# New orders and slots for the tiles of the first two images in a two-layer attention kernel

## The chip, the cores and the metric

The kernel runs on one core of a Trainium2 chip. Its metric is the device time of one execution in microseconds, the median of several runs. Five engines work from queues of their own, each in its written order: TensorE (PE; PEld are its weight loads), VectorE (DVE), ScalarE (ACT), GpSimd (POOL) and SyncE (SP, which issues the DMAs here). They meet through semaphores.

## The reference

Input: eight images x of 256 channels by 1024 positions, float32. Two attention layers follow each other.

```
layer 0:  q = Wq x + bq,  k = Wk x + bk   (32 channels each),  v = Wv x + bv (256)
          energy[n, m] = sum_c q[c, n] k[c, m];  attn = softmax over m
          x1 = gamma * (v attn^T) + x
layer 1:  h = group_norm(x1, 32 groups) * w + b
          q, k, v = 1x1 convolutions of h (256 channels)
          attn = softmax(q^T k / 16);  out = Wp (v attn^T) + bp
          y = x1 + out
```

## The kernel before, in words

Matmuls that need float32 accuracy are done in three passes: a number is split into a high part (`fp32r`) and a low part, and hi*hi, hi*lo and lo*hi are added (`three`, L596 to L598). ScalarE or GpSimd makes the high parts, DVE or GpSimd the low ones.

PSUM has four slots of 128 x 1024 float32 (`ring`). Slots 2 and 3 hold the output of the running "phase" (probabilities times values, four banks), slots 0 and 1 take everything else. An entry of the work list is a tile such as `("keys", image, k)`. It goes to the slot named in `PLACE`, or to the one given out longest ago, and PE fills it only after the entry before it in that slot has been read (`BEFORE`, `wait_read`). Readers are:

- `scores` (layer 0, two matmuls, L606): DVE takes the row maximum (L1058), then ScalarE the exponential in place with its sum (L841). Eight of these and a logarithm give the `shift`, one row of numbers that PE turns (L635) and ScalarE copies into the query tile (L851).
- `keys` (layer 0, transposed, two matmuls, L616): ScalarE's exponential (L817) and high part (L831), DVE's low part (L1075). The result is one of eight steps of the phase, 12 matmuls.
- `qk` (projection of layer 0): DVE and ScalarE write parts into `q4` and `k4` (L1022, L1023, L1030, L879, L884).
- `value0`: values of layer 0. Image 0's are first copied (L867, and L1044 for tiles 2 and 3, `keep_values`) and split by GpSimd (L525, L526); those of later images are split by ScalarE (L869) and DVE (L1010).
- `query`, `value1`, `logits`: layer 1; the query's parts are L861 and L1005. `norm`, `weights`, `bias`: small products.

The order is written out by hand as a list of `Step`s. In a step PE fills `tile`, then `early`, does the first banks of the phase's matmuls, fills `sides`, does the other banks, and fills `late`. ScalarE follows tile, early, sides, late. DVE follows early before the tile's low part, and sides and late after it. `first_image` has 14 steps: `start`, `scores` (scores of image 0 and its last values), `opening` (qk of image 1, shift, first weights), then `steps[0]` to `steps[7]` with keys tile k of image 0 and, from k = 2 on, phase step k - 2, and `s8` to `s10`. In it the scores of image 1 are done too: tiles 0 to 5 in `steps[3]` to `steps[7]`, with two (2 and 3) in `steps[5]`. Keys are in slot 0 and these scores in slot 1. `second_image` has the keys of image 1 beside the scores of image 2 and the first layer-1 work; e8, e9 and e10 are its steps after the last keys tile. The rest is a loop over images that stays as it is.

GpSimd has its own order at the end of its program (`small_things`, `first_values0`, `first_split_x`, `bias_rows`, `residual0`, ...). `first_split_x` splits image 1's x into `h_hi`, `h_lo` (L463, L465), which PE reads for image 1's qk; `residual0` is L497. SP issues the load of image 2 when `residual0(0)` is done.

Of the kernel before, what the change touches and what calls it, by code (L numbers as in the profile page):

```python
# [14 lines left out]
TILES = N // P  # L15
# [19 lines left out]
class Step:  # L35
# [15 lines left out]
    def entries(self):  # L51
# [4 lines left out]

PLACE = {("qk", 1, 0): 2, ("value0", 0, 2): 3, ("bias", 0, 0): 3}
PLACE.update({("weights", 0, m): 3 for m in range(4)})
PLACE.update({("keys", 0, k): 0 for k in range(2, TILES)})
PLACE.update({("scores", 1, k): 1 for k in range(7)})  # L60
PLACE.update({("qk", 2, 1): 1, ("value0", 2, 0): 1, ("scores", 2, 0): 0, ("scores", 2, 1): 0, ("value0", 2, 1): 1,
              ("query", 0, 0): 0, ("scores", 2, 2): 1, ("query", 0, 1): 0, ("scores", 2, 3): 1, ("scores", 2, 4): 1})
PLACE.update({("keys", 1, k): slot for k, slot in ((4, 0), (5, 0), (6, 1), (7, 1))})
PLACE.update({("value0", 1, m): m // 2 for m in range(3)})
PLACE.update({("value1", 0, 0): 2, ("value1", 0, 1): 3, ("value1", 0, 2): 2, ("scores", 2, 5): 3,
              ("value1", 0, 3): 2})

# [12 lines left out]
def tiles(kind, image, ks):  # L80
    return [(kind, image, k) for k in ks]


def first_image():

    start, scores, opening = Step(slots=(0, 1, 2, 3)), Step(slots=(0, 1, 2)), Step()
    start.sides = tiles("qk", 0, (0, 1)) + tiles("value0", 0, (0, 1))
    scores.late = tiles("scores", 0, (0, 1, 2)) + tiles("value0", 0, (2,)) + tiles("scores", 0, (3,))
    scores.late += tiles("value0", 0, (3,)) + tiles("scores", 0, (4, 5, 6, 7))
    scores.keep_values = True  # L90
    opening.opening = True
    opening.sides = tiles("qk", 1, (0, 1))
    opening.late = tiles("shift", 0, (0,)) + tiles("weights", 0, (0,))
    steps = [Step(("keys", 0, k), (0, 0, k - 2) if k >= 2 else None) for k in range(TILES)]
    steps[0].rest = True
    steps[1].late = tiles("weights", 0, (1, 2, 3))
    steps[1].take_weights = True
    for k, s in enumerate((3, 4, 5, 6, 7)):
        steps[s].early = tiles("scores", 1, (k + (s > 5),))
    steps[5].late = tiles("scores", 1, (3,))  # L100
    steps[4].sides = tiles("value0", 1, (0,))
    steps[6].sides = tiles("value0", 1, (1,))
    steps[6].x_lo_end = 2, 0
    s8, s9, s10 = Step(None, (0, 0, 6)), Step(None, (0, 0, 7)), Step(("keys", 1, 1))
    s8.early = tiles("scores", 1, (6, 7))
    s8.early_log = 1
    s8.late = tiles("value0", 1, (2,))
    s9.sides = tiles("shift", 1, (0,))
    s9.late = tiles("keys", 1, (0,))
    s10.sides = tiles("bias", 0, (0,))  # L110
    s10.x_lo_end = 2, 1
    return [start, scores, opening] + steps + [s8, s9, s10]


def second_image():

    steps = [Step(("keys", 1, k), (0, 1, k - 2), 1) for k in range(2, TILES)]
    steps += [Step(None, (0, 1, 6)), Step(None, (0, 1, 7)), Step()]
    s2, s3, s4, s5, s6, s7, e8, e9, e10 = steps
    s2.banks_first = 2  # L120
    s2.sides = tiles("value0", 1, (3,))
    s2.statistics = (0, 0), (0, 1)
    s3.sides = tiles("qk", 2, (0,))
    s4.banks_first = 3
    s4.sides = tiles("qk", 2, (1,))
    s4.low_first = True
    s5.banks_first = 2
    s5.sides = tiles("value0", 2, (0,)) + tiles("norm", 0, (0,))
    s5.late = tiles("norm", 0, (1,))
    s6.early = tiles("scores", 2, (0,))  # L130
    s6.early_in_front = True
    s7.banks_first = 2
    s7.sides = tiles("scores", 2, (1,))
    s7.hidden_mid = e8.hidden_lo = 0
    e8.banks_first = 2
    e8.sides = tiles("value0", 2, (1,))
    e8.late = tiles("query", 0, (0,)) + tiles("scores", 2, (2,))
    e9.banks_first = 4
    e9.sides = tiles("scores", 2, (3,)) + tiles("query", 0, (1,))
    e10.sides = tiles("value1", 0, (0,)) + tiles("scores", 2, (4,)) + tiles("value1", 0, (1,))  # L140
    ones = [Step(("logits", 0, k), (1, 0, k - 2) if k >= 2 else None) for k in range(TILES)]
    ones[0].late = tiles("value1", 0, (2,)) + tiles("scores", 2, (5,))
    ones[1].late = tiles("value1", 0, (3,))
    ones[2].statistics, ones[3].statistics = ((1, 0),), ((1, 1),)
    ones[3].late = tiles("scores", 2, (6,))
    ones[4].sides = tiles("value0", 2, (2,))
    ones[4].late = tiles("scores", 2, (7,))
    ones[4].log = ones[5].shifts = 2
    ones[5].sides = tiles("value0", 2, (3,)) + tiles("norm", 1, (0,))
    ones[5].late = tiles("norm", 1, (1,))  # L150
    ones[6].sides = tiles("shift", 2, (0,))
    ones[5].split_x, ones[5].x_lo_end, ones[6].x_lo_mid = 3, (3, 0), (3, 1)
    return steps + ones
# [61 lines left out]


STEPS = first_image() + second_image() + [step for i in range(2, IMAGES) for step in turn(i)] + last_image()
RING_NO, SLOT, BEFORE, TILE_NO, PHASE_NO = {}, {}, {}, {}, {}
_given, _last = {slot: -1 for slot in range(4)}, {}
# [66 lines left out]
def build(nc, x, wqk_t, bqk, bk0, wv0_t, bv0, gamma, norm_w, norm_b, wq, bq, wk, bk, wv, bv, wp_t, bp,  # L286
          ident, group, y):
    with ExitStack() as ctx:
# [84 lines left out]
        def x_split(i):  # L373

            return (h_hi, h_lo) if i == 1 else (x_hi, x_lo)
# [23 lines left out]
        S = {name: ctx.enter_context(nc.semaphore(name)) for name in SEMAPHORES}  # L399
        x_loaded = (S["x_loaded0"], S["x_loaded1"])  # L400

        def x_loads(i):

            return 16 * (i // 2 + 1)
# [44 lines left out]
        def _(pool):  # L449
# [3 lines left out]
            def link(ins):  # L453
                links[0] += 1
                ins.then_inc(S["pool_link"], 1)
                pool.wait_ge(S["pool_link"], links[0])

            def first_split_x():
                pool.wait_ge(x_loaded[1], x_loads(1))
                hi, lo = x_split(1)  # L460
                for half in range(HALVES):
                    cols = half_cols[half]
                    G.tensor_copy(hi[:, :, cols], x_in[1][:, :, cols]).then_inc(S["x_hi"], 1)  # L463
                    pool.wait_ge(S["x_hi"], 2 + half + 1)
                    G.tensor_tensor(lo[:, :, cols], x_in[1][:, :, cols], hi[:, :, cols].bitcast(F32),  # L465
                                    ALU.subtract).then_inc(S["x_split"], 1)
# [40 lines left out]
            def small_things():  # L507
                for j in range(2):
                    G.memset(k4[j][96:98].bitcast(F32), 1.0).then_inc(S["small_ready"], 1)
                    pool.wait_ge(S["small_ready"], j + 1)  # L510
                pool.wait_ge(S["wv0_loaded"], 16 * 4)
                link(G.tensor_copy(wv0_hi[:], wv0_f))
                G.tensor_tensor(wv0_lo[:], wv0_f, wv0_hi[:].bitcast(F32), ALU.subtract).then_inc(S["v0_weights"], 1)
                G.tensor_copy(ident_r[:], ident_s[:]).then_inc(S["small_ready"], 1)
                link(G.tensor_scalar(gbv[:], bv0_s[:], gamma_s[:], None, ALU.mult))

            def first_values0(m):

                two = slice(2 * m, 2 * m + 2)
                if m < 2:  # L520
                    pool.wait_ge(S["value0_taken"], m + 1)
                else:
                    pool.wait_ge(S["value0_kept"], 1)
                src = kept_values(m)
                link(G.tensor_copy(v0_hi[:, two], src))  # L525
                G.tensor_tensor(v0_lo[:, two], src, v0_hi[:, two].bitcast(F32),  # L526
                                ALU.subtract).then_inc(S["value0_first"], 1)
# [16 lines left out]
            G.memset(unit[:], 1.0).then_inc(S["ones_ready"], 1)  # L544
            pool.wait_ge(S["ones_ready"], 3)
            small_things()
            for m in range(2):
                first_values0(m)
            first_split_x()
            pool.wait_ge(S["shift_ready"], 1)  # L550
            bias_rows()
            for m in (2, 3):
# [238 lines left out]
        def _(act):  # L791
# [45 lines left out]
            def row_sums(entry):  # L837
                _, i, k = entry
                slot = SLOT[entry]
                act.wait_ge(S["scores_max"], i * TILES + k + 1)  # L840
                activation(ring[:, slot], ring[:, slot], ACT.Exp, bias=neg_max0[:, k:k + 1],  # L841
                           accum_out=row_sum0[:, k:k + 1]).then_inc(S["scores_exp"], 1)
# [5 lines left out]
            def shift_rows(entry):  # L848
                _, i, _ = entry
                act.wait_ge(S["ring_ready"], RING_NO[entry] + 1)  # L850
                copy(q4[i % 2][96:98], ring[0:2, SLOT[entry]]).then_inc(S["shift_read"], 1)  # L851
# [375 lines left out]
```

## Time and profile before

| | us |
|---|---|
| three runs | 801.15, 801.2, 802.32 |
| median | 801.2 |
| profiled execution, its own time | 802.13 |
| its span in the profile | 800.3 |
| mean granted TensorE clock | 0.994 |

The profile is of one execution. Its times are counted from the start of the span; L numbers are lines of the kernel. A row of the order of time has the start, the duration, the engine, the line and operation, output<-inputs, and in brackets how long the engine had been idle and whose end it waited for. Several equal instructions in a row are merged (xN).

### The profile page before, as it was taken

What the parts mean: (1) busy time and instruction counts of PE and PEld (TensorE: products, weight loads), DVE (VectorE), ACT (ScalarE), POOL (GpSimd) and SP (SyncE); (2) the same over time, 40 slices, a digit from 0 to 9 for tenths busy, and PEclk for the clock granted to TensorE, in tenths of its full rate; (3) what the DMA queues carried; (4) which work ended last, traced back from release to release, by engine and by line L of the source; (5) the groups of instructions that cost most, each with busy time, mean ns of one, the idle gap of its engine ahead of it and who ended that gap; (6) DMA issues with size and microseconds to landing.
All of it is one profiled execution on the core that took longest, in us unless ns stands there. A gap on an engine that the chain in (4) does not pass through costs nothing.

```text
span 800.3 us, 9813 instructions
## 1 busy us (share of the span) xinstructions
PE 784.6 (98%) x3816; PEld 648.0 (81%) x3816; DVE 550.7 (69%) x790; ACT 468.1 (58%) x603; POOL 163.7 (20%) x147
## 2 busy tenths in 40 slices
PE   9889999999999999999999999999999999999998
PEld 8668787887888878888788877888778888888886
DVE  5866767778568775787657876577856756385564
ACT  4875655568556675557645676455864556445343
POOL 4730061023100231002410042102301024101120
PEclk9999999999999999999999999999999999999999
DMA  6010010002000030001100011000100001000101
GB/s 185 0 54 1 1 53 1 1 2 105 1 1 1 0 106 1 1 1 52 54 1 1 0 53 53 2 0 1 53 1 1 0 1 53 1 0 1 53 1 52
DMA packets 10365, 18.98 MB, mean 24 GB/s; under 512 B 2128, under 2 KB 3920, under 8 KB 10320
## 3 DMA queue, kind: packets, MB, share of 16 engines
q1 hardware_dynamic: 10320, 18.36, 6.6%
q8 instruction: 30, 0.49, 0.3%
q14 instruction: 15, 0.12, 0.1%
HBM read 9.97 MB, written 8.39 MB: 23 GB/s over the span
## 4 chain that ended last, share of the span: by engine, by line
PE 86%; DVE 9%; ACT 3%; issue 1%; POOL 0%; ACTq 0%; DVEq 0%; POOLq 0%
PE ring L596 26%; PE ring L598 26%; PE ring L597 26%; PE ring L606 4%; PE ring L616 3%; DVE res L1111 2%; DVE h_lo L963 1%; DVE pt_lo L1075 1%; DVE q L1030 1%; PE ring L593 1%; ACT ring L841 1%; DVE k L1022 1%; DVE k L1023 1%; ACT prob L817 1%; DVE neg_max L1058 1%
## 5 line engine op out<-in xcount | busy, mean ns | idle before, releaser
L596 PE MATMUL ring<-pt_hi,v_hi 128*128 128x512 f32 x480 | 190.1, 396 | 0.1
L598 PE MATMUL ring<-pt_hi,v_lo 128*128 128x512 f32 x480 | 188.8, 393 | 0.0
L597 PE MATMUL ring<-pt_lo,v_hi 128*128 128x512 f32 x480 | 188.6, 393 | 0.0
L820 ACT ACTIVATE prob<-ring,neg_max 128x1024 f32<-128x1024 f32 x64 | 71.5, 1117 | 157.1 <-DVE neg_max L1061 157.1
L1060 DVE TENSOR_REDUCE neg_raw<-ring 128x1 f32<-128x1024 f32 x64 | 78.1, 1221 | 59.4 <-PE ring L598 59.2
L504 POOL TENSOR_TENSOR v_lo<-v_f,v_hi 128x512 fp32r<-128x512 f32 x28 | 37.7, 1347 | 386.9 <-ACT v_hi L858 386.9
L598 PEld LDWEIGHTS ring<-pt_hi,v_lo 128*128 128x128 f32 x480 | 90.7, 189 | 20.1
L596 PEld LDWEIGHTS ring<-pt_hi,v_hi 128*128 128x128 f32 x480 | 90.6, 189 | 19.1 <-issue 1.6
L597 PEld LDWEIGHTS ring<-pt_lo,v_hi 128*128 128x128 f32 x480 | 90.9, 189 | 17.8
L1075 DVE TENSOR_TENSOR pt_lo<-prob,pt_hi 128x1024 fp32r<-128x1024 f32 x64 | 82.1, 1283 | 32.9 <-ACT pt_hi L831 32.7
L1058 DVE TENSOR_REDUCE neg_max<-ring 128x1 f32<-128x1024 f32 x64 | 77.6, 1222 | 36.8 <-PE ring L606 36.8
L1078 DVE SCALAR_TENSOR_TENSOR pt_lo<-prob,row_inv,pt_hi 128x1024 fp32r<-128x1024 f32 x64 | 83.0, 1297 | 15.0 <-ACT pt_hi L834 15.0
L841 ACT ACTIVATE ring<-ring,neg_max 128x1024 f32<-128x1024 f32 x64 | 69.5, 1085 | 40.7 <-DVE neg_max L1058 40.6
L596 PE MATMUL ring<-h_hi,query_hi 128*128 128x512 f32 x224 | 88.0, 393 | 0.0
L597 PE MATMUL ring<-h_lo,query_hi 128*128 128x512 f32 x224 | 87.5, 391 | 0.0
L598 PE MATMUL ring<-h_hi,query_lo 128*128 128x512 f32 x224 | 87.5, 391 | 0.0
L817 ACT ACTIVATE prob<-ring 128x1024 f32<-128x1024 f32 x64 | 65.3, 1020 | 36.4 <-PE ring L616 36.2
L834 ACT ACTIVATE pt_hi<-prob,row_inv 128x1024 fp32r<-128x1024 f32 x64 | 73.8, 1153 | 11.0 <-DVE row_inv L1067 10.8
L831 ACT CAST pt_hi<-prob 128x1024 fp32r<-128x1024 f32 x64 | 67.2, 1051 | 5.3
L606 PE MATMUL ring<-k,q 96*128 96x512 f32 x128 | 42.2, 416 | 9.2 <-ACT ring L841 5.8
L598 PEld LDWEIGHTS ring<-h_hi,query_lo 128*128 128x128 f32 x224 | 42.1, 188 | 8.9
L596 PEld LDWEIGHTS ring<-h_hi,query_hi 128*128 128x128 f32 x224 | 42.1, 188 | 8.9 <-DVE v_lo L1010 0.2
(167 smaller groups left out, 1346.5 us busy)
## 6 DMA issues: line engine op xcount, KB each, us to landing
out_y<-res SPq DMA_DIRECT2D x32, 256.0 KB, 2.2
x_in<-in_x SPq DMA_DIRECT2D x7, 1024.0 KB, 4.9
x_in<-in_x SPq DMA_DIRECT2D x2, 512.0 KB, 5.6
h_f<-in_wv_t SPq DMA_DIRECT2D x1, 256.0 KB, 3.7
res<-in_wq SPq DMA_DIRECT2D x1, 256.0 KB, 6.0
res<-in_wk SPq DMA_DIRECT2D x1, 256.0 KB, 6.3
res<-in_wv SPq DMA_DIRECT2D x1, 256.0 KB, 6.5
res<-in_wp_t SPq DMA_DIRECT2D x1, 256.0 KB, 6.0
```

Of the source, the lines that this page charges most:

```text
L596: mm(out, w_hi, m_hi, start=first, stop=False)
L597: mm(out, w_hi, m_lo, start=False, stop=False)
L598: return mm(out, w_lo, m_hi, start=False, stop=last)
L606: last = mm(out[:, cols], q4[i % 2][0:96, rows], k4[i % 2][0:96, cols], start=True, stop=True)
L817: activation(prob[:, p % PROBS], ring[:, slot], ACT.Exp).then_inc(S["keys_exp"], 1)
L820: activation(prob[:, p % PROBS], ring[:, slot], ACT.Exp, bias=neg_max[:, k % 2:k % 2 + 1], accum_out=row_sum[:, k % 2:k % 2 + 1]).then_inc ...
L834: activation(pt_hi[p % PT][:], prob[:, p % PROBS], ACT.Identity, scale=row_inv[:, k % 2:k % 2 + 1]).then_inc(S["p_hi"], 1)
L841: activation(ring[:, slot], ring[:, slot], ACT.Exp, bias=neg_max0[:, k:k + 1], accum_out=row_sum0[:, k:k + 1]).then_inc(S["scores_exp"], 1)
L1058: V.tensor_reduce(neg_max0[:, k:k + 1], src, AX_X, ALU.max, negate=True).then_inc(S["scores_max"], 1)
L1060: link(V.tensor_reduce(neg_raw[:, k % 2:k % 2 + 1], src, AX_X, ALU.max, negate=True))
L1075: V.tensor_tensor(lo[:], src, hi[:].bitcast(F32), ALU.subtract).then_inc(S["p_split"], 1)
L1078: V.scalar_tensor_tensor(lo[:], src, row_inv[:, k % 2:k % 2 + 1], hi[:].bitcast(F32), ALU.mult, ALU.subtract).then_inc(S["p_split"], 1)
```

## The change

- Step `scores`: value tile (0,3) is made after score tile 5 of image 0, no longer after score tile 3.
- `PLACE`: keys tiles (0,2) to (0,7) go to slot 1, scores (1,0) to (1,6) to slot 0. For image 2 the scores 0 to 4 go to slot 0, and qk (2,1), value0 (2,0) and (2,1) and both query tiles of image 0 to slot 1. value0 (1,0) and (1,1) are in slot 1, (1,2) in slot 0. Entries without a place follow from these: in the first steps of image 1's keys the slots are exchanged, except that keys (1,4) now follows keys (1,3) in its slot, where it followed qk (2,0), and qk (2,1) follows qk (2,0). From there to the end the order is the same with slots 0 and 1 exchanged.
- Scores of image 1: one tile in each of `steps[2]` to `steps[7]`; before, `steps[3]` to `steps[7]` had one and `steps[5]` two.
- e8: scores (2,2) before query (0,0) in `late`.
- GpSimd: image 1's x is split before image 0's values 0 and 1, after a wait for both halves of image 0's split.

```diff
--- before.py
+++ after.py
@@ -56,12 +56,12 @@
 
 PLACE = {("qk", 1, 0): 2, ("value0", 0, 2): 3, ("bias", 0, 0): 3}
 PLACE.update({("weights", 0, m): 3 for m in range(4)})
-PLACE.update({("keys", 0, k): 0 for k in range(2, TILES)})
-PLACE.update({("scores", 1, k): 1 for k in range(7)})
-PLACE.update({("qk", 2, 1): 1, ("value0", 2, 0): 1, ("scores", 2, 0): 0, ("scores", 2, 1): 0, ("value0", 2, 1): 1,
-              ("query", 0, 0): 0, ("scores", 2, 2): 1, ("query", 0, 1): 0, ("scores", 2, 3): 1, ("scores", 2, 4): 1})
+PLACE.update({("keys", 0, k): 1 for k in range(2, TILES)})
+PLACE.update({("scores", 1, k): 0 for k in range(7)})
+PLACE.update({("value0", 1, 0): 1, ("value0", 1, 1): 1, ("value0", 1, 2): 0})
 PLACE.update({("keys", 1, k): slot for k, slot in ((4, 0), (5, 0), (6, 1), (7, 1))})
-PLACE.update({("value0", 1, m): m // 2 for m in range(3)})
+PLACE.update({("scores", 2, k): 0 for k in range(5)})
+PLACE.update({entry: 1 for entry in (("qk", 2, 1), ("value0", 2, 0), ("value0", 2, 1), ("query", 0, 0), ("query", 0, 1))})
 PLACE.update({("value1", 0, 0): 2, ("value1", 0, 1): 3, ("value1", 0, 2): 2, ("scores", 2, 5): 3,
               ("value1", 0, 3): 2})
 
@@ -85,8 +85,8 @@
 
     start, scores, opening = Step(slots=(0, 1, 2, 3)), Step(slots=(0, 1, 2)), Step()
     start.sides = tiles("qk", 0, (0, 1)) + tiles("value0", 0, (0, 1))
-    scores.late = tiles("scores", 0, (0, 1, 2)) + tiles("value0", 0, (2,)) + tiles("scores", 0, (3,))
-    scores.late += tiles("value0", 0, (3,)) + tiles("scores", 0, (4, 5, 6, 7))
+    scores.late = tiles("scores", 0, (0, 1, 2)) + tiles("value0", 0, (2,)) + tiles("scores", 0, (3, 4, 5))
+    scores.late += tiles("value0", 0, (3,)) + tiles("scores", 0, (6, 7))
     scores.keep_values = True
     opening.opening = True
     opening.sides = tiles("qk", 1, (0, 1))
@@ -95,9 +95,8 @@
     steps[0].rest = True
     steps[1].late = tiles("weights", 0, (1, 2, 3))
     steps[1].take_weights = True
-    for k, s in enumerate((3, 4, 5, 6, 7)):
-        steps[s].early = tiles("scores", 1, (k + (s > 5),))
-    steps[5].late = tiles("scores", 1, (3,))
+    for k in range(6):
+        steps[k + 2].early = tiles("scores", 1, (k,))
     steps[4].sides = tiles("value0", 1, (0,))
     steps[6].sides = tiles("value0", 1, (1,))
     steps[6].x_lo_end = 2, 0
@@ -134,7 +133,7 @@
     s7.hidden_mid = e8.hidden_lo = 0
     e8.banks_first = 2
     e8.sides = tiles("value0", 2, (1,))
-    e8.late = tiles("query", 0, (0,)) + tiles("scores", 2, (2,))
+    e8.late = tiles("scores", 2, (2,)) + tiles("query", 0, (0,))
     e9.banks_first = 4
     e9.sides = tiles("scores", 2, (3,)) + tiles("query", 0, (1,))
     e10.sides = tiles("value1", 0, (0,)) + tiles("scores", 2, (4,)) + tiles("value1", 0, (1,))
@@ -544,9 +543,10 @@
             G.memset(unit[:], 1.0).then_inc(S["ones_ready"], 1)
             pool.wait_ge(S["ones_ready"], 3)
             small_things()
+            pool.wait_ge(S["x_split"], 2)
+            first_split_x()
             for m in range(2):
                 first_values0(m)
-            first_split_x()
             pool.wait_ge(S["shift_ready"], 1)
             bias_rows()
             for m in (2, 3):
```

## Rows read from the trace of the kernel before

**Rows 1.** The page's first part, busy time of each engine: us, share of span, instructions.

```profile
PE 784.6 (98%) x3816; PEld 648.0 (81%) x3816; DVE 550.7 (69%) x790; ACT 468.1 (58%) x603; POOL 163.7 (20%) x147
```

**Rows 2.** Waits of PE from 0 to 180 us: total us, times, longest.

```profile
PE ring L606 <- ACT ring L841: 5.8, 7, 2.1
```

**Rows 3.** Three stretches of 30 us: busy us of each engine, granted clock, DMA share, GB/s.

```profile
20.00:50.00 30.00, 26.77 (x121) 20.70 (x122) 23.75 (x26) 24.92 (x36) 21.09 (x19) 0.94 0.10 36
50.00:80.00 30.00, 27.47 (x134) 21.64 (x133) 17.35 (x20) 18.29 (x25) 1.55 (x2) 0.94 0.00 1
80.00:110.00 30.00, 29.60 (x139) 24.14 (x139) 21.84 (x36) 19.48 (x23) 6.90 (x8) 0.94 0.00 1
```

**Rows 4.** Instructions in order of time, 22 to 42 us: start, us, engine, line.

```profile
23.89 2.35 POOL L465 TENSOR_TENSOR h_lo<-x_in,h_hi 128x1024 fp32r<-128x1024 f32 x1
...
25.29 0.73 PE L606 MATMUL ring<-k,q 96*128 96x512 f32 x2 [1.04 <-ACT ring L841]
...
26.38 0.54 PE L596 MATMUL ring<-h_hi,wqk_hi 128*128 128x512 f32 x1 [0.36 <-ACT ring L841]
...
27.36 1.09 ACT L841 ACTIVATE ring<-ring,neg_max 128x1024 f32<-128x1024 f32 x1
...
29.24 0.17 DVE L1085 TENSOR_TENSOR shift_pair<-shift,shift_pair 128x8 fp32r<-128x8 f32 x1
...
31.03 0.68 ACT L879 ACTIVATE q<-ring,bqk_s 64x512 fp32r<-64x512 f32 x1 [1.26 <-PE ring L598]
...
31.73 1.00 ACT L851 CAST q<-ring 2x1024 fp32r<-2x1024 f32 x1
...
32.88 1.16 PE L616 MATMUL ring<-q,k 98*128 98x512 f32 x4 [0.49 <-ACT q L851]
...
34.42 1.27 POOL L526 TENSOR_TENSOR v_lo<-x,v_hi 128x512 fp32r<-128x512 f32 x1
...
35.80 3.43 POOL L497 TENSOR_SCALAR x<-x_in,unit,gbv 128x1024 f32<-128x1024 f32 x2
...
37.50 1.05 ACT L831 CAST pt_hi<-prob 128x1024 fp32r<-128x1024 f32 x1
...
37.53 0.73 PE L616 MATMUL ring<-q,k 98*128 98x512 f32 x2 [0.89 <-ACT prob L817]
...
38.59 1.72 DVE L1075 TENSOR_TENSOR pt_lo<-prob,pt_hi 128x1024 fp32r<-128x1024 f32 x1 [0.41 <-ACT pt_hi L831]
```

**Rows 5.** The same, 40 to 69 us.

```profile
40.84 0.63 PE L616 MATMUL ring<-q,k 98*128 98x512 f32 x2
...
44.51 0.63 PE L616 MATMUL ring<-q,k 98*128 98x512 f32 x2
...
49.80 0.73 PE L616 MATMUL ring<-q,k 98*128 98x512 f32 x2
...
53.94 0.73 PE L606 MATMUL ring<-k,q 96*128 96x512 f32 x2 [0.20 <-ACT ring L841]
...
57.23 1.07 PE L606 MATMUL ring<-k,q 96*128 96x512 f32 x2 [2.09 <-ACT ring L841]
...
63.68 0.73 PE L616 MATMUL ring<-q,k 98*128 98x512 f32 x2
...
67.83 1.20 PE L606 MATMUL ring<-k,q 96*128 96x512 f32 x4 [0.21 <-ACT ring L841]
```

**Rows 6.** The same, 90 to 94 us.

```profile
92.41 0.73 PE L616 MATMUL ring<-q,k 98*128 98x512 f32 x2 [0.40 <-DVE q L1030]
```

**Rows 7.** The same, 112 to 132 us.

```profile
120.46 2.71 DVE L1108 SCALAR_TENSOR_TENSOR x<-ring,gamma_s,x 128x512 f32<-128x512 f32 x4
...
121.83 0.74 PE L606 MATMUL ring<-k,q 96*128 96x512 f32 x2 [1.69 <-ACT ring L841]
...
126.59 1.28 DVE L1005 SCALAR_TENSOR_TENSOR query_lo<-ring,query_b,query_hi 128x1024 fp32r<-128x1024 f32 x1 [2.28 <-ACT query_hi L861]
...
128.56 0.39 PE L596 MATMUL ring<-h_hi,query_hi 128*128 128x512 f32 x1
```


## The prediction

> **What bounds the kernel now.** I read the page's engine shares first. TensorE (PE) is busy 98% of the 800.3 us span, its weight loads 81% beside it, DVE 69% [rows 1], so time comes back only where PE pauses or runs at the lower clock. The waits of PE up to 180 us name one large source: score tiles that stood for ScalarE's exponential of an earlier score tile, 5.8 us in 7 waits [rows 2]. The table by stretches has the granted clock: 0.94 in each of 20 to 50, 50 to 80 and 80 to 110 us [rows 3]. Six per cent of 30 us missing, at a level that is half, is 1.8 / 0.5 = 3.6 us at 1.2 GHz in each stretch; a PE that works through it loses half, some 1.7 us.
>
> The order of time shows where. At 25.29 PE waits 1.04 us for an exponential, at 26.38 another 0.36, and the projection then starts at half clock; its second half reaches ScalarE only at 31.03, after 1.26 us idle there, which carries the shift row to 31.73 and keys tile (0,0) to 32.88 [rows 4]. At 53.94 the second score tile of its step waits, and at 57.23 the next stands 2.09 us; half clock follows again, and keys tile (0,7) starts at 63.68 [rows 5]. Keys tile (1,4) waits 0.40 us for a bank of image 2's qk at 92.41 [rows 6]. Scores tile (2,3) waits 1.69 us at 121.83 [rows 7]. These are the places that the diff touches.
>
> **The opening.** Nothing is added or removed; value tile (0,3) goes behind score tile 5. Before, it kept score tile 4 back. Now tile 4 may start as soon as the exponential of tile 1 has let its slot go, at 21.2 by my replay instead of 22.1, and DVE's maxima run on without a gap. But the 12 value matmuls (1.4 us, 0.117 apart) now hold tile 6 back to 24.2, so the last exponential starts at 27.3 rather than 27.36: about 0.1 us. More comes from image 1's qk: its slot is freed by score tile 5, 0.6 us sooner (25.8 against 26.38), and PE has worked almost without a pause in the 3 us before, so I expect full clock: 12 matmuls in 2.8 us, done at 28.6 instead of 30.8. What is late next is the shift: its pair is ready at 29.24 + 0.17 = 29.41, less 0.1 [rows 4]. ScalarE takes the second query part at 29.45, the row at 30.15, and keys (0,0) starts at 31.3 instead of 32.88: **1.5 us sooner**. Bounds: 0 if the clock drops as before and the exponentials stay, 1.7 at most, as the shift pair holds it.
>
> GpSimd's change gives order, not time. Its four instructions for image 1's x take 6.9 us and ended at 23.89 + 2.35 = 26.24 [rows 4]; now they fill a pause in which GpSimd stood for image 0's first values, and end about 19.4. The use at 25.8 needs their first half, and little later the second. Image 0's first values now come at 23.3, needed at 36. The next thing on GpSimd, the bias rows, waits for the shift. I count nothing. Cover gone, it would cost 0.1 to 0.4 us at the second qk half. SP's load of image 2 waits for the residual at the end of this queue, and lands long before its use.
>
> **Steps of image 0 (keys on one slot, scores on the other, one score per step).** Keys (0,2) no longer waits for the exponential of keys (0,1), but score (1,0) in the same step now does: the 0.89 us [rows 4] stays as a pause in front of the score. The score tile moved up costs 0.47 us there (two matmuls 0.235 apart) and is saved three steps on. Then something new. Score (1,1) needs the slot of score (1,0), whose maximum stands on DVE behind the low part of keys (0,1). That low part starts after ScalarE's copy, 37.50 + 1.05 less 1.5, so at 37.0; it takes 1.2 to 1.72 us (the same row, with GpSimd's residual beside it [rows 4]). Then maximum and exponential: from one score tile on PE to the next that waits for it is 57.23 - 53.94 = 3.29 us, of which 0.77 is PE's own [rows 5]. So score (1,1) starts at 38.7 + 0.05 + 2.5 = 41.3, and PE, free at 39.6, **pauses 1.6 us** (bounds 1.1 to 2.2). Image 1's values queue behind it. That eats the gain of the opening: the step that began at 44.51 [rows 5] begins at 41.3 + 0.47 + 2.74 = 44.5, but with one more score tile done.
>
> Now the steps without a second score. A step of keys, score and values is 44.51 - 40.84 = 3.67 us, 2.74 of it the values; one with a value tile of image 1 is 49.80 - 44.51 = 5.29 [rows 5]. Before, from 49.80 to 63.68, PE took 13.88 us for two such steps, 8.96, plus one score tile 0.47; the other 4.4 us are the two score waits (0.4 and 2.3 with the pipeline's tail) and 1.7 of half clock. Keys (0,5) starts at 49.8 again, and keys (0,7) at 49.8 + 3.67 + 5.29 + 0.1 = 58.9: **4.8 us sooner** (bounds 3.0, with one half-clock period, to 5.4). Does the single score slot hold the pace? A step's exponential lets the slot go 67.83 - 63.68 = 4.15 us after the step began [rows 5], and the next score is due at 3.67 + 0.47 = 4.14. It fits with nothing to spare; that is the 0.1.
>
> **Steps of image 1.** With keys (1,4) in the slot of keys (1,3), the wait for the qk bank goes: **0.4 us** [rows 6]; the second qk tile takes that slot 2.5 us later, when it is free. Bounds 0 and 0.4.
>
> **Score (2,2) ahead of query (0,0).** Before, ScalarE and DVE did both parts of the query and only then the score, whose exponential let PE go at 121.83 [rows 7]. Now the score is ready three microseconds before the query, and its exponential ends about 117.2 while PE does query and values until 119.95: 1.9 us sooner. Part is given back. DVE's low part of the query ends at 119.8, the evacuation (2.71 us) follows, and then score (2,3). From the evacuation's start to the end of query 1's low part is 126.59 + 1.28 - 120.46 = 7.41 us [rows 7], so that is ready at 127.2; the first logits, at 128.56 before, wait for it. **1.2 us** (bounds 0.6 and 1.9). What is queued behind has slack of over a microsecond, so the gain stays.
>
> **Sum.** 4.8 + 0.4 + 1.2 = 6.4 us. The profiled execution took 802.13 (span 800.3 and 1.8 around it), 0.93 above the median of 801.2. Against itself the sum gives 795.7, against the median 794.8. If that 0.93 is part of a clock period that the change removes anyway, the first holds, else the second. I take the middle, **795.3 us**. From image 1's logits on the order is the old one with slots 0 and 1 exchanged; I cost that at nothing.
>
> **A rule on the shared port.** The low part of keys (0,1) took 1.72 us while GpSimd did the residual, and the two residuals 3.43 [rows 4]. The Trainium skill, SBUF — State Buffer, section "SBUF: two separate sides", says that DVE instructions with two SBUF inputs and GpSimd instructions exclude each other for a whole instruction. By that rule, the trace agrees. It speaks against this change, and the second rival is what it would do here.
>
> **Rivals.** *The clock drops behind the new pause, or where it did before.* A pause of 2.09 us with 0.20 before it was followed by half clock [rows 5], one of 1.69 was not [rows 7]. My 1.6 us pause at 39.7 lies near. One period costs 1.7 us: 797.0; two, 798.7.
>
> *The residual blocks the low part.* Keys (0,1)'s low part is now due at 37.0. GpSimd's last value split (1.27 us [rows 4]) collides with the low part of keys (0,0) from 34.3 to 35.5, ends at 36.8, and the first residual runs 36.9 to 38.1. The low part then starts at 38.1, score (1,1) at 41.9, 0.6 later than I took: 795.9, and with half clock 797.6. The Trainium skill's SBUF — State Buffer page would have it so.
>
> *The third period goes too.* It follows the bias products, which keep PE busy with one-column work. Everything there moves by 5 us; if the clock stays up, 1.7 us more: 793.6.
>
> *No change.* The opening gives nothing and each of the six steps waits 0.6 us for its score slot: 6.4 - 1.5 - 3.6, so 1.3 us are left: 800.4.
>
> *Slower: the single score slot is the bound.* Maximum and exponential of a score must fit between two steps on DVE and ScalarE, each behind two other instructions in order. If the exponential comes more than 1.1 us late in each of the six steps from steps[3] on, the 6.4 are gone; at 1.5 us late PE stands 9 us, and the clock drops in between: 805. For it: release and due time are equal to 0.01 us. Against it: steps[7] had this spacing already and PE waited 0.21 us there [rows 5].
>
> **Chances.** The forecast 45%; port 12%; clock 22%; third period gone 10%; no change 5%; slower 6%. Range 793.0 to 798.9: it leaves out the last two, half of the doubled clock loss and the lower tail. Faster by over 0.2% (1.6 us, what a measurement can tell): 0.87; within: 0.07; slower: 0.06.
>
> **What would show it.** After: qk of image 1 at 25.8 with matmuls 0.23 apart, keys (0,0) near 31.3; a PE wait of 1.1 to 2.2 us on the exponential before score (1,1) near 41; no wait over 0.5 us from there to keys (0,7) at 58.9; granted clock 1.0 in 50 to 80; no wait at keys (1,4); score (2,3) without a wait, then a short one before the first logits. The prediction is wrong if the score waits repeat in each step, if half clock shows in as many periods as before, or if the lead of 5 us at the end of image 0 shrinks before image 1's logits.

## The result, and the profile after

| | kernel before | changed kernel |
|---|---|---|
| median of 6 runs each, same chip | 801.76 us | 795.32 us |
| lowest to highest | 801.15 to 804.05 | 795.07 to 796.15 |
| span of the profiled execution | 800.3 us | 793.9 us |

The ratio is 0.9914 (95% interval 0.9900 to 0.9929): 0.86% faster, 6.4 us by the medians and by the spans. The forecast was 795.3. The total was right; one step of it was wrong, and two things made that good: an event that stood among the rivals, and a start that happened to be earlier in this profile.

First the three stretches of 30 us, as in [rows 3]: busy us of PE, PEld, DVE, ACT, POOL, granted clock, DMA share, GB/s, of the changed kernel.

```profile
20.00:50.00 30.00, 25.65 (x118) 20.37 (x118) 23.77 (x26) 25.21 (x37) 18.29 (x19) 0.94 0.10 36
50.00:80.00 30.00, 29.52 (x158) 23.93 (x157) 19.57 (x29) 19.98 (x27) 2.75 (x3) 1.00 0.00 1
80.00:110.00 30.00, 30.00 (x148) 24.73 (x148) 24.39 (x33) 19.85 (x24) 12.25 (x10) 1.00 0.00 1
```

Before, each stretch had 0.94: one period of 3.4 us at 1.2 GHz in each. Now only the first has one. PE is busy 29.52 and 30.00 us where it was busy 27.47 and 29.60. In the first stretch it is busy less than before, 25.65 against 26.77.

The waits of PE from 0 to 180 us, as in [rows 2]: total us, times, longest.

```profile
PE ring L606 <- ACT ring L841: 2.7, 5, 1.5
PE ring L635 <- DVE shift_pair L1085: 1.4, 1, 1.4
```

Waits of score tiles for an exponential fell from 5.8 us to 2.7. A new one of 1.4 us stands before the shift row. The order of time has both, and answers to [rows 4]:

```profile
19.46 0.72 PE L606 MATMUL ring<-k,q 96*128 96x512 f32 x2 [0.21 <-ACT ring L841]
20.59 0.73 PE L606 MATMUL ring<-k,q 96*128 96x512 f32 x2 [0.41 <-ACT ring L841]
21.72 0.96 PE L606 MATMUL ring<-k,q 96*128 96x512 f32 x2 [0.40 <-ACT ring L841]
22.48 0.41 PE L596 MATMUL ring<-wv_hi,x_hi 128*128 128x256 f32 x1
...
25.04 1.28 PE L606 MATMUL ring<-k,q 96*128 96x512 f32 x4
25.89 2.36 DVE L1058 TENSOR_REDUCE neg_max<-ring 128x1 f32<-128x1024 f32 x2 [1.95 <-PE ring L606]
26.16 0.40 PE L596 MATMUL ring<-h_hi,wqk_hi 128*128 128x512 f32 x1
...
30.51 0.64 PE L635 MATMUL ring<-ident_r,shift_pair 128*2 128x128 f32 x8 [1.38 <-DVE shift_pair L1085]
...
32.34 1.17 PE L616 MATMUL ring<-q,k 98*128 98x512 f32 x4 [0.27 <-ACT q L851]
...
36.99 0.73 PE L606 MATMUL ring<-k,q 96*128 96x512 f32 x2 [0.43 <-ACT prob L817]
37.69 3.35 POOL L496 TENSOR_SCALAR x<-x_in,unit,gbv 128x1024 f32<-128x1024 f32 x2
38.06 1.91 DVE L1075 TENSOR_TENSOR pt_lo<-prob,pt_hi 128x1024 fp32r<-128x1024 f32 x1 [0.42 <-ACT pt_hi L831]
...
42.39 0.73 PE L606 MATMUL ring<-k,q 96*128 96x512 f32 x2 [1.46 <-ACT ring L841]
```

The half clock of this part did not go, it moved. It now lies on value tile (0,3): its matmuls start 0.21 us apart (22.48, 22.69) where 0.12 is their full-speed spacing. The tile takes 2.6 us, and DVE stands 1.95 us before score 6. Image 1's qk at 26.16 runs at full speed and is done early, but then waits 1.38 us for the shift. Keys (0,0) starts at 32.34 instead of 32.88. But the whole profile runs 0.6 us ahead already at the first score tile (16.20, before 16.81), so the opening gained nothing.

Those 0.6 us are not the change's. PE begins with 60 idle matmuls, and they took less time; the kernel before first, then the changed one:

```profile
0.98 9.45 PE L593 MATMUL ring<-ones 128*128 128x128 f32 x60 [0.98 <-POOL unit L544]
```

```profile
0.97 8.86 PE L593 MATMUL ring<-ones 128*128 128x128 f32 x60 [0.97 <-POOL unit L543]
```

PE runs 6 or 7 of them a us at first, and 11 or 12 from 6.2 us on in the one profile, from 5.0 us on in the other. In the 14 profiles of this study that moment lies anywhere between 3.9 and 6.6 us, whichever version runs, and the first score tile starts between 15.68 and 17.00 us, always 6.4 us after the idle matmuls' end. A run-to-run difference of up to 1.3 us comes from there.

The steps of image 0 and the places in image 1 and e8, as in [rows 5 to 7]:

```profile
50.98 0.73 PE L616 MATMUL ring<-q,k 98*128 98x512 f32 x2
...
54.76 0.63 PE L616 MATMUL ring<-q,k 98*128 98x512 f32 x2
...
60.30 0.73 PE L616 MATMUL ring<-q,k 98*128 98x512 f32 x2 [0.25 <-DVE v_lo L1010]
...
86.91 0.63 PE L616 MATMUL ring<-q,k 98*128 98x512 f32 x2
...
114.39 0.63 PE L606 MATMUL ring<-k,q 96*128 96x512 f32 x2
...
119.36 0.73 PE L606 MATMUL ring<-k,q 96*128 96x512 f32 x2
120.34 1.28 DVE L1005 SCALAR_TENSOR_TENSOR query_lo<-ring,query_b,query_hi 128x1024 fp32r<-128x1024 f32 x1 [2.28 <-ACT query_hi L861]
121.77 0.47 PE L596 MATMUL ring<-h_hi,query_hi 128*128 128x512 f32 x1 [0.24 <-DVE query_lo L1005]
```

From keys (0,5) to (0,7) PE takes 9.32 us instead of 13.88, with no wait at a score tile. Keys (1,4) at 86.91 and score (2,3) at 114.39 do not wait. The first logits wait 0.24 us for the query's low part.

The lead over the kernel before, read along the matmuls of the two profiles (start of the tile's first matmul; the last row is the same matmul in both, the 76th from the end):

| at | before | after | lead, us |
|---|---|---|---|
| first score tile | 16.81 | 16.20 | 0.6 |
| keys (0,0) | 32.88 | 32.34 | 0.5 |
| keys (0,5) | 49.80 | 50.98 | -1.2 |
| keys (0,7) | 63.68 | 60.30 | 3.4 |
| bias products | 77.4 | 74.0 | 3.4 |
| keys (1,3) | 87.21 | 82.28 | 4.9 |
| keys (1,4) | 92.41 | 86.91 | 5.5 |
| score (2,3) | 121.83 | 114.39 | 7.4 |
| first logits | 128.56 | 121.77 | 6.8 |
| logits (0,2) | 137.42 | 130.74 | 6.7 |
| near the end | 779.70 | 773.30 | 6.4 |

### The profile page after: what moved, and what is told of

The parts are those of the page before. It is cut to its first block, busy times and chain, and to the rows that moved or that the text cites. A ratio compares the mean times of both kernels' runs of the same rounds, so it can differ in the third digit from the quotient of the medians.

```text
span 793.9 us, 9812 instructions
## 1 busy us (share of the span) xinstructions
PE 780.9 (98%) x3816; PEld 645.5 (81%) x3816; DVE 550.3 (69%) x790; ACT 468.8 (59%) x603; POOL 165.8 (21%) x147
## 4 chain that ended last, share of the span: by engine, by line
PE 85%; DVE 9%; ACT 4%; issue 1%; POOL 0%; ACTq 0%; DVEq 0%; POOLq 0%
PE ring L596 26%; PE ring L598 25%; PE ring L597 25%; PE ring L606 4%; PE ring L616 3%; DVE res L1111 2%; DVE pt_lo L1075 2%; DVE h_lo L963 1%; ACT ring L841 1%; DVE q L1030 1%; PE ring L593 1%; DVE k L1022 1%; ACT pt_hi L831 1%; DVE k L1023 1%; ACT prob L817 1%
## 5 line engine op out<-in xcount | busy, mean ns | idle before, releaser
L1060 DVE TENSOR_REDUCE neg_raw<-ring 128x1 f32<-128x1024 f32 x64 | 78.2, 1223 | 59.0 <-PE ring L598 58.9
L597 PEld LDWEIGHTS ring<-h_lo,query_hi 128*128 128x128 f32 x224 | 42.1, 188 | 8.6
```

What stands on the lines that cost most here:

```text
L597: mm(out, w_hi, m_lo, start=False, stop=False)
L1060: link(V.tensor_reduce(neg_raw[:, k % 2:k % 2 + 1], src, AX_X, ALU.max, negate=True))
```

## The experiments

Numbers with an interval are ratios to the kernel before, run on the same chip. First each part alone, to see whether they add up.

**The opening alone.**

```diff
-scores.late = tiles("scores", 0, (0, 1, 2)) + tiles("value0", 0, (2,)) + tiles("scores", 0, (3,))
-scores.late += tiles("value0", 0, (3,)) + tiles("scores", 0, (4, 5, 6, 7))
+scores.late = tiles("scores", 0, (0, 1, 2)) + tiles("value0", 0, (2,)) + tiles("scores", 0, (3, 4, 5))
+scores.late += tiles("value0", 0, (3,)) + tiles("scores", 0, (6, 7))
```

> The kernel before, with value tile (0,3) behind score tile 5 and nothing else. My theory (the opening is worth next to nothing): the 12 value matmuls only move from one score tile to another, and a half-clock period falls either on them or on image 1's qk; keys (0,0) starts within 0.5 us of its old time, and the whole is within 0.5 us of before. The rival, my prediction's own step: 1.5 us faster, as the clock stays up and keys (0,0) starts near 31.3.

Measured 0.9990 (0.9978 to 1.0002), 802.26 us. From the first score tile (16.07) to keys (0,0) (32.20) it takes 16.13 us; the kernel before takes 16.07. My prediction's step is refuted for this kernel.

**GpSimd's order alone.**

```diff
+pool.wait_ge(S["x_split"], 2)
+first_split_x()
 for m in range(2):
     first_values0(m)
-first_split_x()
```

> The kernel before, with GpSimd splitting image 1's x before image 0's first values. Theory: GpSimd's work is off the path in this place, so within 0.4 us of before, and the two halves of x ready some 6 us earlier. Rival: qk of image 1 had waited for this split (it ended 0.14 us before its first use), so up to 0.5 us faster; or the values come too late for the first phase step and it is slower by up to 1 us.

Measured 1.0003 (0.9991 to 1.0015). Nothing, as the theory said.

**Slots and one score tile per step alone**: the changed kernel with the opening, GpSimd's order and e8 as before.

```diff
-scores.late = tiles("scores", 0, (0, 1, 2)) + tiles("value0", 0, (2,)) + tiles("scores", 0, (3, 4, 5))
-scores.late += tiles("value0", 0, (3,)) + tiles("scores", 0, (6, 7))
+scores.late = tiles("scores", 0, (0, 1, 2)) + tiles("value0", 0, (2,)) + tiles("scores", 0, (3,))
+scores.late += tiles("value0", 0, (3,)) + tiles("scores", 0, (4, 5, 6, 7))
...
-e8.late = tiles("scores", 2, (2,)) + tiles("query", 0, (0,))
+e8.late = tiles("query", 0, (0,)) + tiles("scores", 2, (2,))
...
-pool.wait_ge(S["x_split"], 2)
-first_split_x()
 for m in range(2):
     first_values0(m)
+first_split_x()
```

> The changed slots and one score tile per step, but the opening, GpSimd's order and the order in e8 as before. Theory: this is the body of the gain. 2.1 us of waiting and 1.7 us of half clock between keys (0,5) and keys (0,7), 0.4 us at keys (1,4), less 1.2 to 1.6 us of a new wait before score (1,1): 3 to 5 us faster. Rival, if the bias products' half clock goes by itself with the new place in time and not by chance: 1.7 us more, 5 to 6.5 us.

Measured 0.9961 (0.9944 to 0.9978), 3.1 us faster. In its profile the lead at keys (0,7) is 2.9 us, at keys (1,4) 3.5. The half clock at the bias products is still there (from 78.2 us). So this is the body of the gain, and in this profile the bias products' period did not go though they stood 3 us earlier.

**e8 alone.**

```diff
-e8.late = tiles("query", 0, (0,)) + tiles("scores", 2, (2,))
+e8.late = tiles("scores", 2, (2,)) + tiles("query", 0, (0,))
```

> The kernel before, with only score (2,2) and query (0,0) exchanged in e8. Theory: score (2,3) no longer waits 1.69 us, 0.6 us of it is given back before the first logits because DVE's evacuation stands behind the query's low part: 1.2 us faster. Rival: nothing is given back, 1.9 us; or all of it, as ScalarE and DVE are the bound there, 0.

Measured 0.9980 (0.9971 to 0.9988), 1.6 us faster. In the profile the lead beyond its start is 1.4 us at score (2,3), 0.7 at the first logits and 0.6 at logits (0,2). Part is given back, as forecast. The 1.6 us are in part a difference in clock: all 12 runs of this kernel have 0.994, six of the 30 of the kernel before have 0.991. Against the other 24 alone, at 0.993 and 0.994, the medians are 801.4 and 802.2, 0.8 us apart.

The four parts alone make 0.8 - 0.2 + 3.1 + 1.6 = 5.3 us, each uncertain by 0.7 to 1.4 us; together they gave 6.9 by the ratio, and 5.9 in the repeat further down. That is no contradiction, but it led to the question whether the opening does something in the presence of the rest.

**The changed kernel with the opening's old order.**

```diff
-scores.late = tiles("scores", 0, (0, 1, 2)) + tiles("value0", 0, (2,)) + tiles("scores", 0, (3, 4, 5))
-scores.late += tiles("value0", 0, (3,)) + tiles("scores", 0, (6, 7))
+scores.late = tiles("scores", 0, (0, 1, 2)) + tiles("value0", 0, (2,)) + tiles("scores", 0, (3,))
+scores.late += tiles("value0", 0, (3,)) + tiles("scores", 0, (4, 5, 6, 7))
```

> The changed kernel with value tile (0,3) back behind score tile 3. Theory from the run of the opening alone: the opening's order is worth nothing, so within 0.5 us of the changed kernel (795 to 796 where before is 801.8, that is 6.4 us faster than before). Rival, my prediction's step: 1.5 us slower than the changed kernel.

Measured 0.9957 (0.9940 to 0.9973), 798.12 us: by the ratios 2.4 to 3.4 us slower than the changed kernel (0.9914, and 0.9927 in its repeat), and both theories missed it. The opening itself is no slower with the old order: in seven profiles with the old order keys (0,0) starts 15.63 to 16.09 us after the first score tile, in four with the new order, without the idle matmuls that come below, 16.13 or 16.14. This kernel's profiled execution was 795.94 us at mean clock 0.998. The five others were 797.4 to 799.6 at 0.993 to 0.995. One half-clock period takes 1.7 us of 796, that is 0.002 of the mean clock: they had two or three periods, the first had one, and the changed kernel's six runs had 0.997 to 1.000. Query (0,0) also waits 0.90 us in that profile, for the low part of value tile (2,1). Two more profiles of the same kernel were to show where the other periods lie:

> The changed kernel with value tile (0,3) back behind score tile 3, one look, to see where its half-clock periods lie when it has more than one. Its runs had mean clocks of 0.993 to 0.998, that is one to three periods, where the changed kernel had none or one. Theory: the second and third lie behind the pause at score (1,1) near 41 to 44 us and at the bias products near 77; in the opening there is one in both kernels. Rival: the opening has two of them.

> The same kernel as the look before it, a second look for the same question: the same two theories, and in addition that the pause at query (0,0) (1.15 us in one profile, none in another) comes and goes with which of GpSimd's residual and DVE's low part starts first.

They took 797.59 and 798.04 us. The same stretch from 74 us on, the first of the two:

```profile
74.00:94.00 20.00, 20.00 (x99) 16.71 (x98) 15.00 (x26) 12.96 (x15) 0.00 (x0) 0.91 0.00 1
```

the second:

```profile
74.00:94.00 20.00, 20.00 (x93) 17.21 (x92) 14.14 (x24) 11.62 (x14) 0.00 (x0) 0.83 0.00 0
```

0.91 of 20 us is one period, 0.83 two. Both lie at the bias products and the values behind them, and cost 1.6 and 3.1 us (from keys (1,1) to (1,3) 10.42 and 11.97 us instead of 8.85). Neither has a period behind the pause at score (1,1): that part of the theory is wrong. The pause at query (0,0) appeared in neither; what decides it stands below, with the idle matmuls.

**DVE takes the maximum of score (1,0) first.**

```diff
-pending = None
+pending = held = None
...
-if now.tile and not logits and not now.low_first:
+if held and now.early:
+    follow(held)
+    held = None
+if now.tile == ("keys", 0, 1):
+    held = now.tile
+elif now.tile and not logits and not now.low_first:
     follow(now.tile)
```

> The changed kernel, but DVE takes the maximum of score (1,0) before the low part of keys (0,1). Theory: the wait of 1.46 us before score (1,1) is this place in DVE's queue (and GpSimd's residual, which held the low part to 1.91 us); the maximum starts 2.1 us sooner, the wait all but goes, and score (1,1) and all behind come 1.2 to 1.6 us sooner. Rival: ScalarE is the bound there (the high part of keys (0,2) stands before the exponential until 40.0), so only 0.3 to 0.8 us come back; or the low part, now later, holds the second phase step, 0.

Its order of time around the place:

```profile
37.71 1.23 DVE L1058 TENSOR_REDUCE neg_max<-ring 128x1 f32<-128x1024 f32 x1
38.85 3.28 DVE L1075 TENSOR_TENSOR pt_lo<-prob,pt_hi 128x1024 fp32r<-128x1024 f32 x2
...
39.89 1.08 ACT L841 ACTIVATE ring<-ring,neg_max 128x1024 f32<-128x1024 f32 x1
...
41.14 0.73 PE L606 MATMUL ring<-k,q 96*128 96x512 f32 x2 [0.25 <-ACT ring L841]
```

The maximum starts at 37.71 instead of 39.88, the wait falls from 1.46 to 0.25 us, and score (1,1) comes 1.25 us sooner. The cause of the pause is shown. But the whole is no faster: 0.9922 (0.9905 to 0.9938). In the profile the lead is 1.2 us until the bias products and -0.4 behind them: a half-clock period came back there, and four of six runs have 0.995 or 0.996.

**Idle matmuls in the opening's pauses**, into the half of slot 3 that value tile (0,3) overwrites later.

```diff
+FILL = {("scores", 0, 2): 0, ("value0", 0, 2): 1, ("scores", 0, 3): 2, ("scores", 0, 4): 2}
...
 for entry in now.late:
     fill(entry)
+    if entry in FILL:
+        keep_busy(ring[:, 3, HALF:N], FILL[entry])
```

> The changed kernel with 5 passes of idle matmuls (10 of 128 columns, 0.3 us a pass, into a free half bank) in PE's pauses between score tiles 2 to 5 of image 0. Theory: the half clock in the opening comes from these pauses; with them filled the granted clock is 1.0 from 15 to 50 us, value tile (0,3) takes 1.4 us instead of 2.6, and keys (0,0) starts 0.8 to 1.2 us sooner: the step that my prediction had at 1.5 us. Rival: the clock stays up and nothing is won, because the order of score tiles on DVE and ScalarE is the bound.

Its order of time:

```profile
19.24 0.73 PE L607 MATMUL ring<-k,q 96*128 96x512 f32 x2
19.81 0.61 PE L594 MATMUL ring<-ones 128*128 128x128 f32 x4
...
23.49 1.09 PE L607 MATMUL ring<-k,q 96*128 96x512 f32 x4
...
28.78 0.64 PE L636 MATMUL ring<-ident_r,shift_pair 128*2 128x128 f32 x8 [0.82 <-DVE shift_pair L1088]
...
30.59 1.16 PE L617 MATMUL ring<-q,k 98*128 98x512 f32 x4 [0.27 <-ACT q L854]
```

The granted clock stays at 1.0 to 76 us. Keys (0,0) starts 14.6 us after the first score tile instead of 16.1: **1.5 us sooner**, the very size of the step that the prediction had. So the step's arithmetic was right and its condition, full clock, was not met. No run fills the pauses of the old order, so whether the new order has any part in the 1.5 us, or the clock alone brings them, is not shown. The whole was 0.9925 (0.9910 to 0.9939), again no better: this profile loses 1.55 us to a half-clock period at the bias products, and 1.15 us at query (0,0).

That second loss is between GpSimd and DVE. The changed kernel first, then the one with idle matmuls; GpSimd's residual of layer 1 and DVE's low part of keys (1,7):

```profile
101.19 4.42 POOL L488 TENSOR_SCALAR res<-x,unit,bp_s 128x1024 f32<-128x1024 f32 x2
...
103.43 1.26 DVE L1075 TENSOR_TENSOR pt_lo<-prob,pt_hi 128x1024 fp32r<-128x1024 f32 x1 [1.13 <-ACT pt_hi L831]
```

```profile
100.99 3.35 POOL L489 TENSOR_SCALAR res<-x,unit,bp_s 128x1024 f32<-128x1024 f32 x2
...
103.27 2.14 DVE L1078 TENSOR_TENSOR pt_lo<-prob,pt_hi 128x1024 fp32r<-128x1024 f32 x1 [1.19 <-ACT pt_hi L834]
```

In the one GpSimd is 1.07 us longer and DVE is not held; in the other DVE is 0.88 us longer and GpSimd is not. The inputs and the order are the same. The Trainium skill, SBUF — State Buffer, section "Who interferes with whom", calls the shared port pair an exclusive lock, and the trace agrees: one of the two runs at its own length, 1.2 us, and the other ends 0.9 to 1.1 us behind it, in all 14 profiles.

Which one wins hangs on very little. The row of GpSimd is two instructions, and the one that meets DVE's is the second (103.36 in the changed kernel, 103.13 in the other). In 12 of the 14 profiles DVE's instruction starts 0.06 to 0.115 us after it and wins all the same; in the two others (the one with idle matmuls just shown, and that of the old opening order) it starts 0.13 and 0.14 us after it and loses. Then value tile (2,1)'s low part is late, and since the change query (0,0) takes that slot: PE waits 0.9 us. This is a cost that the change of slots can bring and the kernel before hadn't shown.

**All together**: the maximum first, value tile (0,3) behind the last score tile, idle matmuls in the pauses.

```diff
-scores.late += tiles("value0", 0, (3,)) + tiles("scores", 0, (6, 7))
+scores.late += tiles("scores", 0, (6, 7)) + tiles("value0", 0, (3,))
...
+FILL = {("value0", 0, 2): 1, ("scores", 0, 3): 2, ("scores", 0, 4): 2, ("scores", 0, 5): 2, ("scores", 0, 6): 2}
```

(with the calls of `keep_busy` and the edit of DVE's order above)

> The changed kernel with the maximum first on DVE, value tile (0,3) behind the last score tile, and idle matmuls (9 passes) in the pauses between score tiles 2 to 7. Theory: no score tile waits for value matmuls any more, DVE's eight maxima run on end, the shift is ready some 1 us sooner than in the kernel before and the clock stays up: 1.2 to 1.6 us from the maximum and 1 to 2 us from the opening, together 2.2 to 3.6 us faster than the changed kernel. Rival: the filling matmuls are themselves in the way of score tiles and cost what they win: 1 to 1.6 us.

Measured 0.9906 (0.9890 to 0.9922), 794.57 us: by the medians 0.8 us below the changed kernel, so the 2.2 to 3.6 us expected were missed. In its profile it is 2.3 us ahead of the changed kernel at keys (0,7), 1.5 from the opening and the rest from the maximum; a half-clock period at the bias products takes 1.5 in its profile. Moving the value tile again brought nothing over the idle matmuls: keys (0,0) starts 14.57 us after the first score tile, where it was 14.60. To compare it directly, both once more on one chip:

> The changed kernel once more, on the same chip as the next. Theory (time differences between runs of one kernel are half-clock periods of 1.7 us and one coin toss of 0.9 to 1.15 us between GpSimd and DVE before query (0,0)): median 795 to 796, granted clock 0.997 to 1.0, and runs at equal clock apart by no more than 1.2 us. Rival: the lead over before is of that one chip, and it is 797 or more here.

> The kernel with the maximum first, the last value tile behind the score tiles and idle matmuls in the pauses, beside the changed kernel. Theory: 2.3 us ahead at keys (0,7) in every run, of which the bias products' half clock takes 1.6 in about half of them: median 0.7 to 1.8 us below the changed kernel. Rival: what it wins comes back as half-clock periods always, within 0.4 us.

Changed kernel 796.03 us, 0.9927 (0.9913 to 0.9940); with all edits 794.22 us, 0.9894 (0.9879 to 0.9908). The intervals do not meet: this version beats both kernels, by 1.8 us and 8.1 us. The part of the expectation on the scatter missed: two runs of the changed kernel at mean clock 0.998 are 795.36 and 797.14, 1.8 apart, where I had allowed 1.2. It left out a third random term, the start of up to 1.3 us told above; whether it made this difference is not shown, as only the first of the two runs was profiled.

## Why the prediction was right, and where it wasn't

- **The opening, 1.5 us: wrong.** The step that failed is the term for value tile (0,3), "1.4 us, 0.117 apart". It took 2.6 us at half clock. Score tile 6, counted from the first score tile, started 8.8 us after it and not 7.4, the last exponential 12.1 us after and not 10.5, and keys (0,0) followed. The full clock that I expected for the qk did come: its 12 matmuls took 2.8 us. But I looked only at the 3 us before the qk and not at what the new order did earlier: taking the value tile away from between scores 3 and 4 left PE with pauses of 0.21, 0.41 and 0.40 us around pairs of score matmuls, and the clock fell at 22 us, under the value tile itself. The idle matmuls show that with full clock the 1.5 us come.
- **GpSimd, 0: right.** Alone it measures 1.0003.
- **The new pause before score (1,1), 1.6 us (1.1 to 2.2): right**, 1.46 us, and from the cause given. The low part that it waits behind took 1.91 us beside the residual, longer than my 1.72; its neighbours took 1.2. It ended 1.95 us after ScalarE's copy, between my 1.7 and the 2.3 of the port rival.
- **The steps to keys (0,7), 4.8 us sooner: the steps themselves right, the sum not.** From keys (0,5) to (0,7) I had 9.1 us and it took 9.32; the single score slot holds the pace, so the rival on the slower side fell. But the lead there is 3.4 us, 2.8 without the head start, because the opening's 1.5 are missing and another 0.5 us in small waits.
- **Keys (1,4), 0.4 us: right**, 0.57 in the profile.
- **e8, 1.2 us: right**, 1.1 us at logits (0,2) (from 5.6 to 6.7), and by the reason given: query 1's low part behind the evacuation, ready at 121.6.
- **The half clock at the bias products: a rival at 10% came true in this profile.** Keys (1,2) to (1,3) took 4.73 instead of 6.28 us. Without it the profile would have shown 4.9 us, not 6.4.
- **The sum: right by luck.** Against the forecast 2.0 us are missing up to keys (0,7). The period that stayed away gave back 1.55, and the earlier start of this profile 0.6, which no step of mine had.

What stays open: why the later period at the bias products comes in some profiles and not in others. In the changed kernel with the old opening order it came in two profiles of three, in the changed kernel in none of two, in all three with idle matmuls, and in the one with the maximum first too. The profiles are too few to say that the opening's order decides it; that this order costs clock somewhere rests on the mean clocks of the runs (0.993 to 0.995 in seven of eight, against 0.996 to 1.000 in all 12 of the changed kernel). Over all 14 profiles of this study the period is there in ten and not in four, and the time at which the bias products start (71.7 to 78.0 us) does not sort them. And the first drop starts between 21.7 and 22.0 us in all four profiles with the new opening order without filling, between 24.4 and 27.1 in the seven with the old.

## What to carry to other kernels

When PE is the bound and its pauses are short, count half-clock periods before microseconds of waiting: each cost 1.5 to 1.7 us here, where the longest single wait was 2.09, and an edit that left PE's work thinner moved such a period instead of removing it. Before adding up leads, subtract the difference at a place that the edit cannot have moved; here that was 0.6 us. Cheap matmuls into a spare bank show within one run whether a step was lost to the clock. With one of two slots given to each kind of tile, look at what stands on the reader engine ahead of the first tile of the new kind; here one exchange on DVE was worth 1.25 us.

## What the runs showed of the hardware

- The mean granted clock tells part of the scatter between runs of one kernel: of 30 runs of the kernel before, 24 had 0.993 or 0.994 (801.1 to 803.7 us) and six 0.991 (803.8 to 804.2). The profile with 0.994 has three stretches of 3.4 us at 1.2 GHz. But the 24 alone spread over 2.6 us, and of the changed kernel's first six runs the slowest (796.15) is the one at 1.000, so the clock is not all of it.
- The 60 idle matmuls at the start took between 8.3 and 9.6 us, by the moment at which PE's pace doubled (3.9 to 6.6 us), and everything behind moved with their end.
- GpSimd against a two-input DVE instruction: the loser took 0.88 or 1.07 us longer. DVE won when it started up to 0.115 us after GpSimd's instruction (12 profiles) and lost when it started 0.13 us or more after it (two).
- The clock fell after three pauses of 0.2 to 0.4 us between pairs of matmuls, with none over 0.41 us from 17 us on. I had watched for long pauses only.
